# Which 16 channels a replicated group of the state-space part holds: 16 neighbours, or every eighth

## The reference, cut to what matters

```python
def _mamba_block(x, ...):
    h = x * rsqrt(mean(x * x) + EPS) * rms_w
    proj = h @ in_W + in_b
    x1, g = proj[..., :D], proj[..., D:]          # D = 256
    x1 = silu(causal_conv(x1, conv_w) + conv_b)   # 4 taps, by channel
    A = -exp(A_log)                               # [D, 16]
    dbc = x1 @ dbc_W + dbc_b
    delta, Bm, Cm = dbc[..., :16], dbc[..., 16:32], dbc[..., 32:]
    delta = softplus(delta @ dup_W + dup_b)
    A_disc = exp(delta[..., None] * A)
    B_x = delta[..., None] * Bm[:, :, None, :] * x1[..., None]
    # over time: hc = A_disc * hc + B_x
    y = einsum('tbdn,btn->btd', hs, Cm)
    return (silu(g) * y) @ out_W + out_b + residual
```

## Time and profile before

| | us |
|---|---|
| median of 3 runs | 1931.85 |
| lowest, highest | 1925.41, 1934.93 |
| the profiled execution | 1930.3 |
| its span, first to last instruction | 1928.5 |
| PE busy | 1756.7 (91%) |
| DVE busy | 1596.1 (83%) |
| POOL busy | 1527.8 (79%) |
| ACT busy | 1252.5 (65%) |

### The profile page before, as it was taken

How to read it: one execution, slowest core, us unless ns; L and a number is a source line. 1 busy time by engine, 2 the same in 40 slices (tenths; PEclk the granted TensorE clock), 3 DMA queues, 4 the chain that set the end, 5 groups by cost and what they waited for, 6 DMA issues and landing times. The chain is left out here.

```text
span 1928.5 us, 73996 instructions
## 1 busy us (share of the span) xinstructions
PE 1756.7 (91%) x30944; PEld 999.4 (52%) x30944; DVE 1596.1 (83%) x2736; ACT 1252.5 (65%) x2339; POOL 1527.8 (79%) x1348
## 2 busy tenths in 40 slices
PE   3798999999999999999999999999999999999862
PEld 1355555555555555555555555555555555555420
DVE  5777998888888897889988898889878798888536
ACT  3566676676676676776776676676766666766630
POOL 1765899878998789878998789888888689987640
PEclk9999999999999999999999999999999999999975
DMA  3114234153313334142332433342331534123321
GB/s 109 29 39 70 45 71 79 37 85 49 66 33 67 72 61 71 41 71 55 68 71 37 87 49 59 74 79 39 67 58 33 100 62 63 30 45 58 54 23 44
DMA packets 95607, 113.14 MB, mean 59 GB/s; under 512 B 42334, under 2 KB 61548, under 8 KB 95276
## 3 DMA queue, kind: packets, MB, share of 16 engines
q1 hardware_dynamic: 95276, 108.41, 31.1%
HBM read 19.22 MB, written 1.05 MB: 11 GB/s over the span
## 5 line engine op out<-in xcount | busy, mean ns | idle before, releaser
L1315 POOL TENSOR_TENSOR AB<-qc,qn 128x512 f32<-128x512 f32 x384 | 494.6, 1298 | 21.4 <-DVE qn L1109 21.4
L1326 POOL TENSOR_TENSOR AB<-AB,rinv 128x512 f32<-128x512 f32 x384 | 402.0, 1062 | 24.5 <-DVE rinv L1132 24.5
L559 PE MATMUL bank<-wqkv,XT 128*128 128x512 f32 x768 | 400.2, 614 | 12.2 <-DVE qn L1109 12.2
L1333 POOL TENSOR_TENSOR Pb<-Pb,p_rden 128x512 f32<-128x512 f32 x192 | 200.1, 1042 | 235.2 <-DVE p_rden L1153 234.1
L848 ACT ACTIVATE qkT<-bank 128x512 f32<-128x512 f32 x384 | 229.2, 597 | 209.3 <-PE bank L584 208.6
L1109 DVE TENSOR_TENSOR qc<-bank,rt 128x512 f32<-128x512 f32 x384 | 261.3, 680 | 123.4 <-ACT sq L839 108.9
L584 PEld LDWEIGHTS bank<-ident,AB 128*128 128x128 f32 x1536 | 181.7, 142 | 181.9 <-issue 119.3
L839 ACT ACTIVATE sq<-bank 128x512 f32<-128x512 f32 x384 | 228.1, 594 | 66.4 <-PE bank L559 57.3
L1109 DVE TENSOR_TENSOR qn<-bank,rt 128x512 f32<-128x512 f32 x384 | 261.4, 681 | 0.0
L584 PE MATMUL bank<-ident,AB 128*128 128x128 f32 x1536 | 241.5, 280 | 13.3 <-ACT qkT L848 6.2
L1116 DVE TENSOR_REDUCE ssq<-sq 128x8 f32<-128x512 f32 x384 | 251.2, 670 | 0.0
(11 more groups left out here) (137 smaller groups left out, 2657.3 us busy)
## 6 DMA issues: line engine op xcount, KB each, us to landing
V<-V SPq DMA_DIRECT2D x672, 64.0 KB, 2.1
rep<-du SPq DMA_DIRECT2D x64, 512.0 KB, 7.3
wqkv<-in_Wqkv SPq DMA_DIRECT2D x36, 256.0 KB, 3.7
XV<-XT SPq DMA_DIRECT2D x96, 64.0 KB, 2.8
wo<-in_Wo SPq DMA_DIRECT2D x6, 512.0 KB, 4.1
BC<-BC SPq DMA_DIRECT2D x8, 256.0 KB
w<-in_W SPq DMA_DIRECT2D x6, 341.0 KB, 3.2
BC<-BC SPq DMA_DIRECT2D x8, 128.0 KB
```

The source lines that it names most:

```text
L559: pe.matmul(R[u % 2][:], XT[:, s % NB, (u % 2) * P:(u % 2 + 1) * P], wqkv[:, (u // 2) * 512:(u // 2 + 1) * 512], start=True, stop=True).th ...
L1315: pool.tensor_tensor(AB[:, n % NAB, :], qc[:, u % 2, :], qn[:, u % 2, :], ALU.add).then_inc(rs_done, 1)
L1326: pool.tensor_tensor(o, o, r, ALU.mult).then_inc(nm_done, 1)
L1333: pool.tensor_tensor(Pb[:, g % 2], Pb[:, g % 2], r, ALU.mult).then_inc(pn_done, 1)
```

## The change

A group n now holds the channels n, n+8, n+16, ... of each block of 128, where it held 16n to 16n+15. The transfer reads `du[n::8]`, that is every eighth partition starting at n, instead of 16 neighbours; it still reads 16 rows of 4 KB and writes each of them 8 times. Partition 8d+z of `rep` now belongs to channel 8d+n. The rows of `Y` therefore come in another order of channels, and whatever meets them is laid out in that order ahead of the launch: the gate's half of `in_W` and `in_b`, the rows of `out_W`, and the decay's `A_log`. The instructions of the five engines, their order and their waits are the same as before.

```diff
@@ replicate @@
-                r = 16 * ROWS16[n]
+                r = ROWS16[n]
                 sp.dma_start(rep[:, (8 * b + n) % NREP].rearrange("p z c t -> p (z c t)"),
-                             du[r:r + 16].rearrange("d (o z) c t -> d o (z c t)", o=1).broadcast_to([16, 8, 2 * DBLK * SEQ]))\
+                             du[r::8].rearrange("d (o z) c t -> d o (z c t)", o=1).broadcast_to([16, 8, 2 * DBLK * SEQ]))\
@@ decay_rows @@
-    return a.reshape(DBLK, 8, 16, 2, 8).transpose(2, 4, 0, 1, 3).reshape(P, DBLK * NST)
+    return a.reshape(DBLK, 16, 8, 2, 8).transpose(1, 4, 0, 2, 3).reshape(P, DBLK * NST)
+
+def sum_order():
+
+    return np.arange(P).reshape(16, 8).T.reshape(-1)
+
+def gate_order(a, axis):
+
+    block = [np.arange(DI + c * P, DI + (c + 1) * P)[sum_order()] for c in range(DBLK)]
+    return np.take(a, np.concatenate([np.arange(DI)] + block), axis)
@@ kernel @@
-    laid["mamba_vecs"], laid["layer_vecs"] = mamba_vectors(given), layer_vectors(given)
+    laid["mamba_vecs"], laid["layer_vecs"] = mamba_vectors({**given, "in_b": gate_order(given["in_b"], 0)}), layer_vectors(given)
     laid["A_rows"] = decay_rows(given["A_log"])
+    laid["in_W"] = gate_order(given["in_W"], 1)
+    laid["out_W"] = given["out_W"].reshape(DBLK, P, DM)[:, sum_order()].reshape(DI, DM)
```

## The result

The changed kernel takes 1885.11 us (median of 4 runs, 1878.74 to 1886.76) against 1931.18 us before (4 runs, 1925.41 to 1934.93). The ratio is 0.9758 with a 95% interval of 0.9724 to 0.9792: 2.4% faster. The profiled execution took 1886.5 us with a span of 1884.7 us, 43.8 us less than the 1928.5 us before.

The account below looks back on a forecast made before the run. Replications were taken to hold back PE's instruction fetches, costing about 59 us; with 13 us staying, 46 us off the profiled 1930.3 gives 1884.3, plus 1.5 for the median: 1886 us, range 1864 to 1920.

Parts of the forecast that it names:

- What bounds the kernel: Main loop: replications hold back PE's instruction fetches and PE runs dry, in all about 59 us.
- breadth: Replication's source: 16 rows spread over all 128 partitions read faster than neighbours, 0.30 in place of 0.61 us a packet.
- The sum: Whole kernel: 59 - 13 = 46 us gained, 1884.3 us profiled, 1886 us as median.
- the 13 us: Loss expected to stay: some 12 us from stalls and low clock behind three replications in a row, 1 us of rests.
- kind 2: One of six kinds of main-loop step, repeating every 6 steps; counted 7.5 us above seven times its fastest step.
- steps of one kind do the same work: Main loop repeats every 6 steps, so time above each kind's fastest step counts as loss: together 53.8 us.
- The second reading: Check on the 59 us: 39.0 us of stalls plus 19 us from 37.7 us at half clock make 58 us.
- the 5 us: Last stall at line 633, up to 3.6 us, and 6.8 us at half clock behind the step windows, counted as 5 us.
- Partial relief: Rival: packets queued behind a replication hold fetches as much; 40% of the 59 us come back, 1908 us; chance 0.11.
- no relief: Rival: nobody waits for the transfer, so at most 7.6 us of landing waits return, 1924 to 1932 us; chance 0.13.
- The rule of turns packet by packet: Skill's rule, siding with the nothing-moves rival: a fetch waits for one packet, not eight, so the time would stay.
- The slower rival: Reading and writing in the same place lengthens packets; at 0.9 us a packet, near 1975 us; chance 0.04.

Follow-up runs that it names:

- the dose: Kernel before, still 16 neighbours, from the second sequence on moving 3.5, 3 or 2 KB of each 4 KB row: 1912.15, 1894.87 and 1887.49 us.
- the five kernels of the experiments that read 16 neighbours: Kernel before with rows cut to 2, 3 or 3.5 KB (1887.49, 1894.87, 1912.15 us), or replications in two halves, apart (1896.13) or directly behind each other (1907.55).
- the three spreads: Changed kernel (every eighth channel, 1885.11 us) and its variants with every second (1880.35 us) and every fourth channel (1884.07 us) as source.

## Why the prediction was right

**What bounds the kernel.** PE runs out of instructions behind replications: confirmed. All 39.0 us of "issue" vanished with the shorter transfer, nothing on PE having changed, and they shrank with the dose while the source stayed (39.0, about 28, about 16 and 6 us at landings of 7.3, 6.6, 6.0 and 4.6 us).

No kernel changed the fetches themselves, but a count of the instructions in the traces settles that the stalls are theirs. There are 63 stalls over 0.55 us that end in "issue": 19 in the kernel before, 44 in the five kernels of the experiments that read 16 neighbours. When such a stall begins, PE has begun exactly 449 + 256 x k instructions (matmuls, weight loads, and the waits of its queue), where k counts the fetches, 16 KB each, that landed before the one that ends the stall. This holds in all 63, and each ends 1.22 to 1.62 us after the next fetch has landed. In the changed kernel PE had never used more than 401 of the 449 when a fetch landed.

Two readings of the prediction were off without changing its sum: its rows have 21 stalls of 1.9 us, not 20 of 2, and in the 8.5 us without a fetch two replications were issued together, not three (`rep<-du x2` at 1198.96).

**The duration.** 0.30 us a packet was forecast and 0.315 measured; landing 4.9 and 4.8 us. The reason given, breadth, was too loose: what counts is not breadth but, as the three spreads show, what lies between neighbours and every second row.

**The sum.** 59 us to gain, 13 to stay, 46 gained was forecast; 43.8 were gained in the profiled executions and 46.1 between the medians. The total is right by two errors that cancel, and that is luck. I expected the 13 us to stay as stalls behind the rows of three replications; none stayed. In the longest case the queue carried no fetch from 952.0 to 958.7 and PE still did not stall: the fetch before had come early (PE had used 180 of its 449 instructions when it began), and when the next one landed, 384 were used. What stayed instead is kind 2, which I had counted with 7.5 us among the stalls. In the changed kernel its sum lies 10.2 us above seven times its fastest step of before (38.97), from POOL's tables and the low clock. The step that failed is "steps of one kind do the same work (their instruction counts agree within a few records)": PE's counts do, but POOL's are x38 in two of the steps and x33 or x34 in the others, before as now, and 42.35 us at 313.62 was such a step.

**The second reading**, 39.0 us of stalls and 19 us of low clock, has the same flaw, and shows where the rest lies. The stalls went in full; of the low clock 8.6 us came back and 10 us stayed; and PE waits 13.2 us longer for POOL's `Pb`. "The clock holds 1.00 through nearly all of the loop" held for the kinds 0, 1, 3, 4 and 5; kind 2 still falls to half the clock after waiting for POOL. Behind the loop the 5 us were right in size only: the stall of 3.6 us went, but 6.8 us at half the clock are there as before (1792.5).

**The rivals.** Partial relief and no relief are excluded by the size. The rule of turns packet by packet (the Trainium skill, "DMA: Bandwidth & Descriptors", section "Queues, rings and completion order") was taken in the prediction as if it spoke of the profile's packets, of which a replication has 8 for each engine. The page's packet is a group of typically 9 to 17 descriptors, and no run here shows how the two compare. If the 8 were one such packet, a single replication without a fetch (5.0 us before, 2.2 us in the changed kernel) and a fetch between two halves would both fit the rule; it would still leave open why two replications together showed none for 8.5 us. That nobody waits for a landing was true and remained without effect.

**The slower rival**, reading and writing in the same place, did not come about: a packet took 0.315 us, near the 0.28 us of the `BC` copy, whose reads and writes are apart, and the run with rows within 32 partitions landed as early.

## What to carry to other kernels

Idle time that ends in "issue" in the middle of a run of instructions without a wait can be a late instruction fetch. Look at which transfer was on the DMA engines just before, even if nobody waits for its data, and count the instructions between the stalls: here they stood at one fixed number beyond the last fetch. A stall can cost a stretch of lowered clock on top of its own length. What the sum of the stalls promises is not all gained, since the engine then meets the next one's limit: 13.2 us came back here as waits for POOL. Before steps are compared as twins, compare every engine's instruction counts. And a transfer whose source is 16 rows should take them from places that do not adjoin: every second row did as well as every eighth.

## What the runs showed of the hardware that was not expected

- How far PE gets without a fetch is a number of instructions, not a time: 449, and 256 more for each fetch landed, in all 63 stalls. So three replications in a row, some 7 us without a fetch, caused no stall in the changed kernel (384 used), while single ones of 4.9 us did before. 14 of the 21 waits of before lie at line 604, where 64 matmuls and their weight loads take 0.84 us.
- Splitting a replication into two transfers of half the row, issued directly behind each other, gave 22 us (1929.14 to 1907.55) although the two moved as slowly as the whole. In three places a fetch came in where the halves meet; how much of the 22 us that is worth is open.
- The time does not fall evenly with the duration of the transfer: 34 us for the first 1.3 us of earlier landing, 5 us for the next 1.4 us.
